# Two transformer layers on one core: loads of the opening on one queue, the second layer's output biases added by GpSimd, one norm's statistics placed behind an item's maxima

## What is computed

```python
attn_in = _adaln(x, cond, ln1_w, ln1_b, g1_w, g1_b, b1_w, b1_b)   # layer norm, then scale and shift per batch
x = _attn(attn_in, attn_in, sa_wq, sa_wkv, sa_wo, sa_bo) + x      # 16 heads of 64, rotary tables
x = _attn(_adaln(x, ...), _ln(context, ...), ca_wq, ca_wkv, ca_wo, ca_bo) + x
x = gelu(_adaln(x, ...) @ ff_w1 + ff_b1) @ ff_w2 + ff_b2 + x
```

```python
x = x + (attend(q, k, v of modulate(_ln(x)) @ W_qkv + b_qkv) @ W_proj + b_proj)
x = x + (attend(modulate(_ln(x)) @ W_q, ctx @ W_k, ctx @ W_v) @ W_out + b_out)
x = x + (gelu(modulate(_ln(x)) @ W_fc1 + b_fc1) @ W_fc2 + b_fc2)
```

## Time and profile before

| | before |
|---|---|
| median of 3 runs (lowest, highest) | 403.86 us (403.36, 404.35) |
| profiled execution, own time | 404.24 us |
| its span, first to last instruction | 402.4 us |
| TensorE clock granted, mean | 1.000 |
| busy: PE | 381.1 us, 95% |
| busy: DVE | 320.5 us, 80% |
| busy: ACT | 296.7 us, 74% |
| busy: POOL | 141.9 us, 35% |
| 16 DMA engines, mean rate | 64 GB/s |
| chain that ended last | PE 52%, DVE 18%, ACT 17%, issue 9%, POOL 2% |

### The profile page before, as it was taken

One profiled execution on the slowest core, in us unless ns is written; L12 is line 12 of the kernel. 1 busy time (PEld: TensorE's weight loads), 2 busy tenths in 40 slices (PEclk: granted clock), 3 DMA queues, 4 the chain that ended last, 5 costly groups with the idle time before them and its releaser, 6 DMA issues.

```text
span 402.4 us, 9925 instructions
## 1 busy us (share of the span) xinstructions
PE 381.1 (95%) x3604; PEld 285.1 (71%) x3604; DVE 320.5 (80%) x702; ACT 296.7 (74%) x1031; POOL 141.9 (35%) x126
## 2 busy tenths in 40 slices
PE   7979999999999999999999998999999999999997
PEld 3557767777777777777777667776768777787664
DVE  4998998988998898989898858673658888788740
ACT  2277886886887777878788795779679787987832
POOL 4364423423634333734245324430264620202010
PEclk9999999999999999999999999999999999999999
DMA  7133333332333233331212110000000000000001
GB/s 230 41 122 115 117 119 99 118 108 100 110 108 132 87 116 113 105 107 55 105 53 80 67 43 26 2 2 1 2 2 3 0 2 4 2 2 2 2 0 54
DMA packets 17348, 25.71 MB, mean 64 GB/s; under 512 B 3630, under 2 KB 6068, under 8 KB 17300
## 3 DMA queue, kind: packets, MB, share of 16 engines
q1 hardware_dynamic: 16548, 24.07, 17.7%
q10 hardware_dynamic: 720, 1.00, 0.8%
q0 software_dynamic: 32, 0.00, 0.0%
HBM read 8.28 MB, written 0.52 MB: 22 GB/s over the span
## 4 chain that ended last, share of the span: by engine, by line
PE 52%; DVE 18%; ACT 17%; issue 9%; POOL 2%; POOLq 0%; DVEq 0%
PE bank L947 41%; ACT prob L424 8%; PE bank L1034 6%; DVE qk L737 4%; PE bank L1242 4%; ACT raw L516 3%; DVE prob L715 2%; DVE qk L728 2%; DVE nmax L825 2%; POOL xn L279 1%; DVE xn L651 1%; PE bank L958 1%; ACT raw L415 1%; POOL rstd L272 1%; DVE x L631 1%
## 5 line engine op out<-in xcount | busy, mean ns | idle before, releaser
L298 POOL TENSOR_TENSOR swp<-swp,small 128x512 f32<-128x512 f32 x62 | 78.9, 1283 | 129.6 <-PE bank L947 96.9
L424 ACT ACTIVATE prob<-bank,nmax 128x128 f32<-128x128 f32 x256 | 91.4, 390 | 1.2 <-DVE nmax L708 1.2
L516 ACT ACTIVATE raw<-bank,nmax 128x128 f32<-128x128 f32 x256 | 72.9, 391 | 11.6 <-DVE nmax L825 11.3
L424 ACT ACTIVATION_READ_ACCUMULATOR prob<-bank,nmax 128x1 f32 x256 | 59.1, 231 | 0.0
L825 DVE TENSOR_REDUCE nmax<-bank 128x4 f32<-128x512 f32 x64 | 41.1, 684 | 17.4 <-PE bank L947 17.4
L708 DVE TENSOR_REDUCE nmax<-bank 128x4 f32<-128x512 f32 x64 | 41.2, 685 | 16.2 <-PE bank L947 16.2
L715 DVE TENSOR_TENSOR prob<-prob,rz 128x512 f32<-128x512 f32 x64 | 49.4, 773 | 2.2
L947 PE MATMUL bank<-hT,wqkv 128*128 128x512 f32 x96 | 49.1, 595 | 0.3 <-DVE qk L728 0.3
L430 ACT ACTIVATE probT<-bank 128x512 f32<-128x512 f32 x32 | 19.1, 597 | 38.4 <-PE bank L1034 38.4
L1034 PEld LDWEIGHTS bank<-small,prob 128*128 128x128 f32 x256 | 28.5, 140 | 26.1 <-DVE prob L715 16.8
L272 POOL TENSOR_TENSOR rstd<-vare,neg_half 128x4 f32<-128x4 f32 x12 | 12.4, 1031 | 95.9 <-DVE vare L643 95.8
(11 more groups left out here) (111 smaller groups left out, 635.5 us busy)
## 6 DMA issues: line engine op xcount, KB each, us to landing
swp<-raw SPq DMA_DIRECT2D x124, 128.0 KB, 2.0
wqkv<-in_wqkv SPq DMA_DIRECT2D x14, 256.0 KB, 3.0
wff<-in_wff SPq DMA_DIRECT2D x4, 256.0 KB, 3.0
x<-in_x SPq DMA_DIRECT2D x2, 256.0 KB, 5.3
wqkv<-in_wqkv ACTq DMA_DIRECT2D x2, 256.0 KB, 5.7
wmod<-in_wmod SPq DMA_DIRECT2D x2, 256.0 KB, 2.8
ctx<-in_ctx SPq DMA_DIRECT2D x1, 384.0 KB, 7.4
ctxT<-in_ctxT SPq DMA_DIRECT2D x1, 384.0 KB, 3.5
```

What stands on the lines that cost most here:

```text
L298: nc.gpsimd.tensor_tensor(four(swp[:, m % 2, f, :]), four(swp[:, m % 2, f, :]), sin[f], ALU.mult).then_inc(rope_sin[f], 1)
L424: last = nc.scalar.activation(prob[:, hh, bcols(u)], S[hh][:, bcols(u)], ACT.Exp, bias=nmax[:, s % 2, hh, u:u + 1], accum_out=zsum[:, s % ...
L516: last = nc.scalar.activation(prob1[:, s % 2, hh, bcols(u)], score_bank(s, hh)[:, bcols(u)], ACT.Exp, bias=nmax[:, s % 2, hh, u:u + 1])
```

## The change

- SP issues in the opening: x half 0, attention weights 0, wswap, x half 1, the rotary tables, weights 1, ctx, weights 2. ScalarE issues only the first part of small and the first modulation weights.
- b_proj, b_out and b_fc2 leave the seeds. They are loaded, repeated over all 128 partitions, into a new tile `rows1` (196 KB) at SP's slot 23. GpSimd adds them to x in place, in six calls of `add_bias(k, half)` for k = 3, 4, 5, each once norm k of that half is normalised. `residual(r, ...)` for r >= 3 waits for that addition besides the matmul's signal, and the two last sums wait for the sixth.
- The first projection matmul of each such accumulation starts it.
- The statistics of norm 2 of half 1 move from slot 1, behind the residual, to slot 2, behind the maxima of item 2 and directly ahead of the aggregation.

```diff
-ROWS = {name: i for i, name in enumerate(["sa_bo", "ca_bo", "ff_b2", "b_proj", "b_out", "b_fc2"])}
+ROWS = {name: i for i, name in enumerate(["sa_bo", "ca_bo", "ff_b2"])}
...
+                elif s == 22:
+                    load(rows1[:, :], row1_in, ld_rows1)
 
             load_x(0)
-            sp.dma_start(wqkv[:, 0, :], wqkv_in[:, 0, :]).then_inc(ld_wqkv[0], 16)
-            sp.dma_start(wswap[:, :], wswap_in).then_inc(ld_swap, 16)
+            load(wqkv[:, 0, :], wqkv_in[:, 0, :], ld_wqkv[0])
+            load(wswap[:, :], wswap_in, ld_swap)
             load_x(1)
-            sp.dma_start(ctx[:, :, :], ctx_in.rearrange("b t d -> t b d")).then_inc(ld_ctx, 16)
+            load(small[:, NFIRST:], small_in[:, NFIRST:], ld_tab)
+            load(wqkv[:, 1, :], wqkv_in[:, 1, :], ld_wqkv[1])
+            load(ctx[:, :, :], ctx_in.rearrange("b t d -> t b d"), ld_ctx)
+            load(wqkv[:, 2, :], wqkv_in[:, 2, :], ld_wqkv[2])
             swap(1)
...
-                if m <= 22:
+                if m <= 23:
                     sp.wait_ge(scores[0], m)
                     loads(m - 1)
...
+            def add_bias(k, half):
+
+                pool.wait_ge(ln_xn[half], k + 1)
+                if k in SPLIT_XN[half]:
+                    pool.wait_ge(ln_xn_dve[half], SPLIT_XN[half].index(k) + 1)
+                pool.wait_ge(ld_rows1, 16)
+                xs = x[:, batches(half), :]
+                row = rows1[:, (k - 3) * P:(k - 2) * P].unsqueeze(1).broadcast_to([P, HALF, P])
+                nc.gpsimd.tensor_tensor(xs, xs, row, ALU.add).then_inc(biased[half], 1)
...
             for j in range(1, SLOTS):
                 mask_keys(0, 0, j)
+            add_bias(3, 0)
             inv_std(1, 2)
             normalise_first(1, 2)
             inv_std(1, 3)
             normalise_first(1, 3)
+            add_bias(3, 1)
             for j in range(1, SLOTS):
                 mask_keys(0, 1, j)
...
                 inv_std(half, 4)
                 normalise_first(half, 4)
+                add_bias(4, half)
             inv_std(0, 5)
             normalise_first(0, 5)
+            add_bias(5, 0)
             inv_std(1, 5)
+            add_bias(5, 1)
...
             load(wmod[:, 0:2 * P], wmod_in[:, 0:2 * P], ld_mod[0])
-            load(small[:, NFIRST:], small_in[:, NFIRST:], ld_tab)
-            load_wqkv(1)
-            load_wqkv(2)
...
                 dve.wait_ge(done, count)
+                if r >= 3:
+                    dve.wait_ge(biased[half], r - 2)
                 nc.vector.tensor_tensor(xs, xs, four(src[:, :]), ALU.add).then_inc(x_sum[half], 1)
...
                 if s == 2:
+                    ln_stats(2, 1)
                     ln_aggregate(2, 1)
...
                     residual(1, 1, W, wo_done, ITEMS)
-                    ln_stats(2, 1)
...
+                dve.wait_ge(biased[1], 3)
                 for i in range(2):
                     dve.wait_ge(acc_done[1], 4 + i)
...
-                if first == 0:
-                    seed("b_fc2" if layer else "ff_b2", dst)
+                if first == 0 and not layer:
+                    seed("ff_b2", dst)
...
                         last = mm(dst[:, bcols(u)], gT[:, c, bcols(u)], wff[:, off + (FF + c) * P:off + (FF + c + 1) * P],
-                                  False, False)
+                                  layer == 1 and c == 0 and u == 0, False)
...
-                seed("b_out" if run // 2 else "b_proj", dst)
...
-                    last = mm(dst[:, bcols(u)], oT[:, run % 2, bcols(u)], weights, False, False)
+                    last = mm(dst[:, bcols(u)], oT[:, run % 2, bcols(u)], weights, u == 0, True)
...
-                    seed("b_fc2", (W, Y)[i], 2 * i, 2 * i + 2)
...
-                            last = mm((W, Y)[i][:, bcols(u)], gT[:, c, bcols(u)], wff[:, off:off + P], False, False)
+                            last = mm((W, Y)[i][:, bcols(u)], gT[:, c, bcols(u)], wff[:, off:off + P], c == 0 and u == 2 * i, c == FF - 1)
```

More of the change, by code:

```diff
@@ L67, in swaps, with build @@
     return (m + 1) // 2
-def build(nc, small_in, x_in, ctx_in, ctxT_in, wqkv_in, wswap_in, wmod_in, wsq_in, wff_in, row_in, out):
+def build(nc, small_in, x_in, ctx_in, ctxT_in, wqkv_in, wswap_in, wmod_in, wsq_in, wff_in, row_in, row1_in, out):
     es = ExitStack()
@@ L90, in build @@
         rows = sb("rows", [len(ROWS), P])
+        rows1 = sb("rows1", [P, 3 * P])
         rest = sb("rest", [len(ROWS), P])
@@ L171, in build @@
         ld_wqkv = [sem(f"ld_wqkv{i}") for i in range(2 * RUN)]
+        biased, ld_rows1 = pair("biased"), sem("ld_rows1")
         presets, padded, row_part, row_moved, dve_link = (
@@ L389, in load @@
                 act.dma_start(dst, src).then_inc(done, 16)
-            def load_wqkv(n):
-                load(wqkv[:, n, :], wqkv_in[:, n, :], ld_wqkv[n])
             def load_table(i, func):
@@ L964, in wait_hT, with seed @@
                     pe.wait_ge(ln_h_dve[half], SPLIT_H[half].index(k) + 1)
-            def seed(name, dst, first=0, end=HALF):
+            def seed(name, dst):
                 pe.wait_ge(row_moved, 48)
                 cols = slice(ROWS[name] * P, (ROWS[name] + 1) * P)
-                mm(four(dst[:, :])[:, first:end, :], ones[:, :],
-                   parts_row[:, cols].unsqueeze(1).broadcast_to([3, end - first, P]), True, False)
+                mm(four(dst[:, :]), ones[:, :], parts_row[:, cols].unsqueeze(1).broadcast_to([3, HALF, P]), True, False)
             def modulation(stage, dst):
@@ L1457, in _packed @@
         "small": small, "x": i["x"], "ctx": i["ctx_768"], "ctxT": i["ctx_768"].reshape(B * P, DC).T,
-        "wqkv": np.stack(wqkv, axis=1), "wswap": wswap, "wmod": wmod, "wsq": wsq, "wff": wff, "row": rows,
+        "wqkv": np.stack(wqkv, axis=1), "wswap": wswap, "wmod": wmod, "wsq": wsq, "wff": wff, "row": rows[0:3], "row1": np.broadcast_to(rows[3:].reshape(-1), (P, 3 * P)),
     }
```

## The result

| | before | after |
|---|---|---|
| median of 7 runs (lowest, highest) | 403.74 us (402.98, 404.35) | 401.61 us (400.80, 403.28) |
| ratio, 95% interval | | 0.995 (0.9937 to 0.9963) |
| profiled execution, span | 402.4 us | 399.5 us |
| TensorE, matmuls | 381.1 us, x3604 | 379.3 us, x3597 |
| GpSimd, busy | 141.9 us, x126 | 149.2 us, x132 |

The change is worth 2.1 us (0.5%, interval 0.37% to 0.63%), where 1.4 us had been forecast.

The account below looks back on a forecast made before the run. The prediction took TensorE, busy 95% of the span, as the bound; -0.75 us at the run ends and -0.65 in the tail, all else 0, made -1.40 from 403.86, say 402.5 us, range 401.7 to 403.5.

Parts of the forecast that it names:

- The three run ends: Ends of the second layer's eight-item runs: each dropped seed gives 0.32 less 0.07 us, so 0.75 us saved.
- the added wait: VectorE's residuals 3 to 5 wait for a second semaphore: 0.07 us each, bounds 0 and 0.10.
- The tail: After the last items: 0.25 us for the fourth projection's seed, 2 x 0.20 for the half-width ones, 0.65 us saved.
- Rival (a): Run ends give nothing as ScalarE's exponentials pace the items; only the tail gains: -0.65, 403.2 us; chance 0.17.
- Statistics: Norm 2's moved statistics: item 2's scores sooner, the norm later, together 0, bounds -0.5 and +0.4 us.
- (b): The moved statistics delay the norm by their 0.4 us: -1.0 in all, 402.9 us; chance 0.16.
- (c): The moved statistics free 0.5 us because GpSimd's half has slack: -1.9 in all, 402.0 us; chance 0.15.
- Additions on GpSimd: Six additions in the second layer, 1.27 us each, cost 0, bounds 0 to 0.3 us in all.
- Rival (d): Additions collide with VectorE, 0.94 us a hit; all six hits make it +4.2, 408.1 us; chance 0.05.
- Loads: Opening: three loads moved from ScalarE's queue to SP's are worth 0, bounds -0.2 and +0.2 us.
- Rival (e): Opening: the single queue delivers late, each microsecond late costing one; chance 0.02.
- the opening unmoved: Expected sign in the trace: the opening stays as it was up to 10.3 us.

Follow-up runs that it names:

- e2_bias: The kernel before with only the second layer's biases moved from seeds to GpSimd additions: 401.55 us, ratio 0.9959.
- e5_noseed: The kernel before without the second layer's seven seeds and with no additions in their place: 123.70 us from layer 1's item 4 to the last sum.
- e3_stats: The kernel before with only norm 2's statistics of half 1 moved behind item 2's maxima: 403.68 us, ratio 1.0003.
- e11_free: The changed kernel with all six biases on GpSimd, without the wait placing layer 0's additions behind VectorE's last rotary sum: 402.55 us, ratio 0.9967.
- e4_noloads: The changed kernel with the opening's loads as before: 401.65 us, ratio 0.9952.
- e8_all6: The changed kernel with layer 0's six seeds gone too, all six biases added by GpSimd, layer 0's additions placed by a wait: 401.05 us, ratio 0.9922.
- e10_split: e8_all6 with one of norm 2's four statistics of half 1 left in slot 1, behind the residual: 401.29 us, ratio 0.9932.
- e6_bf16: The changed kernel with half-width bfloat16 zero matmuls ahead of the last two down-projection groups, 3 rows then 128: +0.42 and +0.11 us in their stretches.
- e9_after: The changed kernel measured once more, unaltered: 402.19 us, ratio 0.9957.

## Why the prediction was right or wrong, step by step

- **Direction and mechanism: right.** The gain comes from TensorE's seeds at the run ends and in the tail, and from nothing else that was measured. The size was not: 2.1 us is half as much again as 1.4.
- **The three run ends: 0.75 forecast, 0.99 measured** (0.33 + 0.33 + 0.33 after, 0.32 + 0.31 + 0.32 in e2_bias). The seed's 0.32 was right: at the first run end the sum starts 0.32 us sooner behind oT (1.98 us instead of 2.30), not 0.25. The 0.07 us of the added wait was wrong: e5_noseed and e2_bias differ by 0.02 us in all, where 0.28 would have been seen, and the separate instruction holds the wait that is long satisfied. I had taken its price from a place where it stood behind the one that ends last.
- **The tail: 0.65 forecast, 1.25 measured** (22.34 - 21.52 = 0.82, 2.12 - 1.69 = 0.43). This is the term that was mis-sized. I took the step from a seed's start to the next start, but a 3-row matmul in saturated TensorE also loses the early weight load, 0.10 us ahead of it and, unless what follows has to wait anyway, 0.10 behind it. The fourth projection's seed gave 0.44 instead of 0.25 (14.69 - 14.25; the wait's 0.07 and the 0.10 ahead), the two half-width ones 0.38 and 0.43 instead of 0.20. At the run ends the step happened to be right: TensorE idles for oT, which the projection loads as its weights, so that load starts with its matmul (310.01) with or without a seed.
- **Rival (a), only the tail gains: fell.** 38.8 of 40 us busy was the right row to go by.
- **Statistics: 0 forecast, +0.12 us measured**, inside the bounds of -0.5 and +0.4. Rivals (b) and (c) both fell; the two effects nearly cancelled as computed. By the time alone (c), 402.0 us, would have looked right, nearer to 401.6 than the forecast; e3_stats shows that its half microsecond does not reach the end.
- **Additions on GpSimd: 0 forecast, 0 measured** in layer 1. Rival (d) is a real mechanism of this kernel, 0.5 to 1.0 us a hit in e11_free, but the six places held no VectorE instruction with two SBUF inputs.
- **Loads: 0 forecast, ratio 0.9996 (0.9985 to 1.0007) measured.** Rival (e) fell. The reason given was too simple: what bounds the opening changes from execution to execution, see below. The sign "the opening unmoved" did not come either (17.90 us to item 0 instead of 18.28), beside a clock that rose at 5.3 us instead of 6.1.
- **Sum.** 0.99 + 1.25 - 0.12 = 2.12 us, and the medians differ by 2.13. The forecast of 1.40 lacked 0.24 (waits) and 0.60 (tail).

## What to carry to other kernels

Price a small matmul by the distance between its neighbours with and without it, weight loads included: one of 3 rows between neighbours of 128 cost 0.42 us, and the same one with all 128 rows 0.11. Work moved to GpSimd cost nothing beside VectorE instructions that read PSUM, and up to 1 us beside those with two SBUF inputs; wait for the right one and place it, and look at what the freed time moves into the next collision. Compare traces by marks item by item before reading a difference of two spans: here 0.8 of 2.9 us was not the change's.

## What the runs showed of the hardware that was not expected

- **The opening's clock.** TensorE's granted clock rose from 1.2 to 2.4 GHz anywhere between 4.0 and 7.3 us in the thirteen profiles, whose warm-up starts at 1.2 to 1.3 us. In some executions it fell back to 1.2 GHz for 3.4 us between 25.5 and 26.0 us (after, e4_noloads, e8_all6, e11_free), once at 10.8 us (e10_split). In after this stands behind 1.4 us in which TensorE idles between 22 and 24 us; but e3_stats and e6_bf16 idle as long there without a fall, so these rows do not say what decides it. Item 1 then took 7.65 us instead of 6.78. By stretch, with the granted clock in the last column but two:

```profile
24.00:26.00 2.00, 1.47 (x21) 1.28 (x19) 1.93 (x10) 0.00 (x0) 0.00 (x0) 0.96 0.78 288
26.00:28.00 2.00, 2.00 (x5) 0.92 (x5) 1.74 (x3) 1.80 (x9) 1.96 (x2) 0.50 0.60 186
28.00:30.00 2.00, 2.00 (x10) 1.65 (x10) 1.75 (x4) 2.00 (x12) 1.99 (x2) 0.69 0.09 33
```

- **The opening's loads.** In e9_after the modulation weights landed 5.0 us after their issue instead of 3.6 in after, and TensorE waited for them, so the same program's opening is once bound by the clock and once by a load:

```profile
6.38 0.58 PE L966 MATMUL bank<-small,wmod 128*128 128x8 f32 x4 [0.86 <-DMA wmod<-in_wmod]
```

- **A change in the number of rows** between 128 and 3, 32 or 64 stopped the early load of the weights behind it; between 128 and 96 it did not. A 3-row bfloat16 matmul of 256 columns cost 0.42 us, the same with 128 rows 0.11.
